# The attention slot of a transformer kernel: masks from the fifth score round on, ScalarE's copies ahead of the output, the input transposed behind the output projection

## The reference, cut to what matters

```
x = x + 0.5 * L0_ffn(layernorm(x))
x = x + L0_attn(layernorm(x))
x = x + 0.5 * L0_ffn(layernorm(x))
x = x + 0.5 * L1_ffn(layernorm(x))
x = x + L1_attn(layernorm(x))
x = x + 0.5 * L1_ffn(layernorm(x))
```

```
h = shift_token(x)                       # half of the channels come from the row before
q, k, v = split(h @ wqkv)                # 8 heads of 64
q = l2norm(q) * qs; k = l2norm(k) * ksc
q, k = rotary_xpos(q, k)
# windows of 128 rows; a row sees its own window and the one before, at most 128 rows back
sim  = (8 q) @ k^T                       # 128 queries x 192 keys for half a window
attn = softmax(where(mask, -max, sim))
x = x + (attn @ v) @ wo
h = layernorm(shift_token(x)) @ w1 + b1
x = x + (a * gelu(g)) @ w2 + b2
```

## Time and profile before

| | us |
|---|---|
| median of 3 runs (lowest, highest) | 3214.93 (3213.61, 3220.47) |
| the profiled execution: its own time | 3218.03 |
| the profiled execution: its span | 3216.0 |
| TensorE busy | 3018.5 (94% of the span) |
| VectorE busy | 2361.8 (73%) |
| ScalarE busy | 1721.1 (54%) |
| GpSimd busy | 1671.5 (52%) |

### The profile page before, as it was taken

The page is one execution under the profiler, slowest core; times in us unless marked ns, Lnnn a source line. Parts: engine busy times, 40 slices in busy tenths (PEclk is TensorE's granted clock), DMA queues, the critical chain, the costliest instruction groups (busy, mean ns, idle before and its releaser), DMA issues.

```text
span 3216.0 us, 98899 instructions
## 1 busy us (share of the span) xinstructions
PE 3018.5 (94%) x35586; PEld 2604.5 (81%) x35586; DVE 2361.8 (73%) x6543; ACT 1721.1 (54%) x4532; POOL 1671.5 (52%) x1839
## 2 busy tenths in 40 slices
PE   6999989989999999999899999999999899999889
PEld 4777878878887888998688878877888788898778
DVE  6777777677777786777677777767777688777766
ACT  4666652266667324665676763237666622454445
POOL 7777740077777224323777771037777444317610
PEclk9999999999999999999999999999999999999999
DMA  4211121021111101000211112102111200100001
GB/s 146 58 42 39 38 81 36 23 62 39 37 38 37 45 20 42 10 11 21 57 39 37 38 37 78 29 25 66 37 38 35 66 26 13 27 1 1 1 14 39
DMA packets 178773, 122.82 MB, mean 38 GB/s; under 512 B 27532, under 2 KB 175336, under 8 KB 178024
## 3 DMA queue, kind: packets, MB, share of 16 engines
q1 hardware_dynamic: 177432, 117.77, 13.6%
q10 hardware_dynamic: 1104, 1.90, 0.2%
HBM read 48.29 MB, written 20.98 MB: 22 GB/s over the span
## 4 chain that ended last, share of the span: by engine, by line
PE 62%; ACT 18%; issue 8%; DVE 8%; DMA 1%; POOL 1%; DVEq 1%; SPq 0%; ACTq 0%; POOLq 0%
ACT prob L1247 14%; PE bank L363 7%; PE bank L365 5%; PE scores L508 5%; PE bank L364 5%; PE scores L363 4%; PE scores L364 4%; PE scores L365 4%; PE bank L478 2%; PE pair_bank L770 2%; PE pair_bank L769 2%; PE pair_bank L768 2%; ACT V L1231 2%; PE scores L714 2%; PE scores L713 2%
## 5 line engine op out<-in xcount | busy, mean ns | idle before, releaser
L2699 POOL TENSOR_TENSOR prob<-prob,rsum 128x384 f32<-128x384 f32 x512 | 467.5, 933 | 282.6 <-DVE rsum L1900 267.2
L1247 ACT ACTIVATE prob<-prob,nmax 128x192 f32<-128x192 f32 x1024 | 452.0, 443 | 290.5 <-DVE nmax L1893 290.4
L1440 ACT ACTIVATE gate<-scores,bias 128x512 f32<-128x512 f32 x192 | 132.2, 689 | 511.4 <-PE scores L365 511.4
L2686 POOL TENSOR_TENSOR rn<-ss,mhalf 128x16 f32<-128x16 f32 x128 | 375.2, 2931 | 10.7
L363 PE MATMUL bank<-wqkv_hi,hT_hi 128*128 128x512 f32 x768 | 338.9, 441 | 8.7 <-DVE hT_lo L1833 3.7
L2693 POOL TENSOR_TENSOR qk<-rot_t 128x512 f32<-128x512 f32 x256 | 322.6, 1278 | 36.1 <-DVE ss L1867 29.7
L2667 POOL TENSOR_TENSOR rstd<-meanvar,eps 128x4 f32<-128x4 f32 x48 | 11.1, 231 | 627.2 <-DVE meanvar L1825 627.2
L1893 DVE CUSTOM_DVE_ANT_0 prob<-scores,masks,rn 128x192 f32<-128x192 f32 x768 | 267.7, 412 | 84.4 <-PE scores L508 83.9
L365 PE MATMUL bank<-wqkv_hi,hT_lo 128*128 128x512 f32 x768 | 305.7, 398 | 0.0
L364 PE MATMUL bank<-wqkv_lo,hT_hi 128*128 128x512 f32 x768 | 302.5, 394 | 0.0
L1853 DVE TENSOR_TENSOR rot_t<-bank,rot 128x512 f32<-128x512 f32 x256 | 176.1, 688 | 163.8 <-ACT qk L1224 156.2
(11 more groups left out here) (338 smaller groups left out, 9662.6 us busy)
## 6 DMA issues: line engine op xcount, KB each, us to landing
Vlo<-V SPq DMA_DIRECT2D x256, 64.0 KB, 2.0
Vhi<-V SPq DMA_DIRECT2D x256, 64.0 KB, 2.0
H<-Y SPq DMA_DIRECT2D x128, 64.0 KB, 1.8
H<-ya SPq DMA_DIRECT2D x128, 64.0 KB, 1.9
yb<-Y SPq DMA_DIRECT2D x128, 64.0 KB, 1.6
HB<-Y SPq DMA_DIRECT2D x32, 256.0 KB, 2.8
HB<-yb SPq DMA_DIRECT2D x32, 256.0 KB, 3.0
raw<-in_L_ffn_wqkv SPq DMA_DIRECT2D x4, 1536.0 KB, 6.9
```

The costliest lines, as they stand in the source:

```text
L1247: ins = e.activation(pb, pb, ACT.Exp, bias=nm[r][:, x:x + 1], scale=-1.0, accum_out=sums[r][:, x:x + 1])
L2686: e.tensor_tensor(rn[u][:, :], ss[:, :], mhalf[:, :], ALU.pow).then_inc(s_plRN, 1)
L2699: e.tensor_tensor(pair, pair, rs[:, 2 * gi:2 * gi + 2].unsqueeze(2).to_broadcast([P, 2, KW]), ALU.mult).then_inc(s_plPN[gi], 1)
```

## The change: what it does

1. **Masks earlier, and one semaphore for all of them.** TensorE counts up a new semaphore `s_peSA` with the last matmul of the fifth of the eight score rounds. By then everything that is written to bank 2 is there (heads 4, 6 and half of head 0). VectorE's `sc_` now waits for `s_peSA` before the first mask and for `s_peS` (all rounds) before the third. The waits for the four transposes of the slot before (`s_pePT`), which stood one before each block, all stand ahead of the first mask now. Each mask counts up `s_dvMX` by itself, and each exponential waits for its own mask and counts up `s_acEX` by itself.
2. **Another order of heads.** Blocks 1 and 2 change places in `PAIRS`; the order of masks and exponentials is that of `EXP_ORDER`. `TURN_BANK` and the order of the transposes, products and copies of the blocks follow.
3. **ScalarE copies qT, V and the input ahead of the output.** `ot_` moves from behind the exponentials to behind the kT copy, and waits also for `hT_lo` of tile T+3.
4. **The input is transposed behind the output projection**, ahead of the q transposes, and into the upper half of bank 6 in place of bank 1. `pv_` waits also for the `hT_lo` that last read that bank.
5. The k projection waits for bank 1 itself, since the input's transposes no longer do it.

```diff
-PAIRS = [(0, 4), (1, 5), (2, 6), (3, 7)]
+PAIRS = [(0, 4), (2, 6), (1, 5), (3, 7)]
+EXP_ORDER = (((0, 1), (1, 1), (0, 0), (1, 0)), ((2, 0), (3, 0), (2, 1), (3, 1)))
-TURN_BANK = (3, 2, 2, 4)
+TURN_BANK = (2, 3, 4, 2)
@@ input_bank @@
-            return bank[2 + T] if spare(run, T) else bank[1]
+            if spare(run, T):
+                return bank[2 + T]
+            return bank[1] if isinstance(T, int) and T < 3 else bank[6][:, 2 * P:4 * P]
@@ TensorE @@
+                                if half_ == 1 and h == 0 and piece == 0:
+                                    ins.then_inc(s_peSA, 1)
...
-                    if gi == 1:
-                        e.wait_ge(s_dvMX[2], G + 1 + OFF)
-                    if gi == 2:
-                        e.wait_ge(s_acPT[1], G + 1 + OFF)
+                    if gi == 0:
+                        e.wait_ge(s_dvMX[2], 2 * G + 2 + OFF)
+                        e.wait_ge(s_dvMX[3], 2 * G + 2 + OFF)
+                    if gi == 3:
+                        e.wait_ge(s_acPT[0], G + 1 + OFF)
@@ TensorE pv_ @@
+                    if inside(T + 3):
+                        e.wait_ge(s_dvHT, G + 4 + OFF)
@@ TensorE slot @@
                         wo_(T - 2, (u - 2) % U)
+                    if inside(T + 3):
+                        ht(T + 3, (u + 3) % U)
                     if inside(T + 1):
                         tr_(T + 1, (u + 1) % U, 0)
                     if inside(T + 2):
                         v_(T + 2, (u + 2) % U)
-                    if inside(T + 3):
-                        ht(T + 3, (u + 3) % U)
@@ ScalarE sc_ @@
-                    e.wait_ge(s_dvMX[gi], G + 1 + OFF)
-                    for i in range(2):
+                    for n, (gi, i) in enumerate(EXP_ORDER[hf]):
...
+                        e.wait_ge(s_dvMX[gi], 2 * G + 1 + n // 2 + OFF)
@@ ScalarE ot_, now behind tr_(T + 1, ..., 1) @@
+                    if inside(T + 4):
+                        e.wait_ge(s_dvHT, G + 5 + OFF)
@@ VectorE sc_ @@
-                    e.wait_ge(s_peS, G + 1 + OFF)
+                    e.wait_ge(s_peSA, G + 1 + OFF)
...
-                    e.wait_ge(s_pePT[gi], G + OFF)
-                    e.sem_inc(s_passed, 1)
+                    for g in range(NG):
+                        e.wait_ge(s_pePT[g], G + OFF)
+                        e.sem_inc(s_passed, 1)
...
+                        if n == 2:
+                            e.wait_ge(s_peS, G + 1 + OFF)
+                            e.sem_inc(s_passed, 1)
```

More of the change, by code:

```diff
@@ L416, in ht @@
                     into = input_bank(run, T)
-                    if not spare(run, T) and not (isinstance(T, int) and T == 0):
+                    if run == DEPTH and isinstance(T, int) and 1 <= T < 3:
                         k_read(T - 1)
@@ L441, in qk_ @@
                         q_read(T - 1)
-                    elif j == 1 and spare(run, T):
+                    elif j == 1 and (not early or spare(run, T)):
                         k_read(T - 1)
@@ L544, in product @@
                         return e.matmul(bank[6 + i][cols, o0:o0 + DH], keys[x][rows, h * DH:(h + 1) * DH], PTs[gi][rows, p0:p0 + DH], start=start, stop=x < 2, skip_group_check=True)
-                    for hf in range(2):
+                    for n in range(2):
                         for x in (2, 3):
-                            for g in range(2):
+                            for gi in (n, n + 2):
                                 for i in range(2):
-                                    product(2 * hf + g, i, x, slice(DH * i, DH * i + DH), hf == 0 and x == 2)
-                    for hf in range(2):
+                                    product(gi, i, x, slice(DH * i, DH * i + DH), n == 0 and x == 2)
+                    for n in range(2):
                         for i in range(2):
                             for x in (0, 1):
-                                for g in range(2):
-                                    ins = product(2 * hf + g, i, x, slice(0, P), False)
-                        ins.then_inc(s_pePV[hf], 1)
+                                for gi in (n, n + 2):
+                                    ins = product(gi, i, x, slice(0, P), False)
+                        ins.then_inc(s_pePV[n], 1)
                 def wo_(T, u):
@@ L1267, in slot @@
                     if inside(T):
+                        sc_(T, u, 0)
                         sc_(T, u, 1)
-                        sc_(T, u, 0)
-                        sc_(T, u, 3)
-                        sc_(T, u, 2)
-                    if inside(T - 1):
-                        ot_(T - 1, (u - 1) % U)
                     if inside(T + 1):
@@ L1280, in slot @@
                     if inside(T):
+                        pt_(T, u, 0)
                         pt_(T, u, 1)
-                        pt_(T, u, 0)
                     if inside(T + 1):
                         tr_(T + 1, (u + 1) % U, 1)
+                    if inside(T - 1):
+                        ot_(T - 1, (u - 1) % U)
                     if inside(T + 3):
@@ L1287, in slot @@
                     if inside(T):
+                        pt_(T, u, 2)
                         pt_(T, u, 3)
-                        pt_(T, u, 2)
                 def iteration(it):
@@ L1887, in sc_ @@
                         e.sem_inc(s_passed, 1)
-                    for i in range(2):
+                    for n, (gi, i) in enumerate(EXP_ORDER[0] + EXP_ORDER[1]):
+                        if n == 2:
+                            e.wait_ge(s_peS, G + 1 + OFF)
+                            e.sem_inc(s_passed, 1)
                         x = 2 * gi + i
@@ L2701, in mask_of @@
                 def mask_of(it):
-                    e.wait_ge(s_dvMX[2], NT * run + U * it - U + 1 + OFF)
-                    e.wait_ge(s_dvMX[3], NT * run + U * it - U + 1 + OFF)
+                    e.wait_ge(s_dvMX[2], 2 * (NT * run + U * it - U + 1) + OFF)
+                    e.wait_ge(s_dvMX[3], 2 * (NT * run + U * it - U + 1) + OFF)
                     odd = it - 2 * (it // 2)
@@ L2723, in slot @@
                     if inside(T):
+                        pn_(T, u, 0)
                         pn_(T, u, 1)
-                        pn_(T, u, 0)
+                        pn_(T, u, 2)
                         pn_(T, u, 3)
-                        pn_(T, u, 2)
                     if inside(T + 2):
```

33 lines of the change are left out of this document (14 added, 19 removed).

## The result

The changed kernel takes 3184.16 us (median of 4 runs, 3179.62 to 3187.18); the kernel before took 3217.7 beside it (3213.61 to 3222.32, 4 runs). The ratio is 0.9894, 95% interval 0.9874 to 0.9914: faster, as forecast, but by 34 us and not by 99. The time lies outside the range of 3102 to 3158. The profiled execution took 3187.18 (span 3185.4), 30.8 less than that of before; clock 0.990 against 0.993.

A forecast was written before the change was run, and what follows sets the result against it. TensorE was taken as leading, losing 0.91 per slot to waits for the V copy and `hT_lo`. 112 full slots x 0.83 (93 us) plus 5 or 6 from edge slots, together 98.5, gave 3116 us, range 3102 to 3158.

The forecast's parts named there:

- the chain: Within a slot, scores, masks, exponentials, output, qT, V, input, `hT_lo` follow one another; shortening it by 0.90 removes both TensorE waits.
- 0.48 + 0.34 + 0.08 = 0.90: Per-slot gain at the V copy: output moved 0.48, exponentials waiting for their own mask 0.34, earlier masks 0.08.
- Two transposes move, none is added: On TensorE, moving the input's transposes was taken as free; only the further wait at `pv_` was charged, 0.05.
- The output costs nothing behind kT: On ScalarE, the 0.48 output fits the 0.97 gap ahead of the square of q; at most 0.48 if not.
- rival A: VectorE's waits ahead of the masks cost 0.23 each, so masks start 0.25 later than before: 3149 us, 12%.
- rival C: VectorE's masks slow down reading PSUM while scores are written; at a pitch of 0.68, 3338 us, 4%.
- The new semaphore: Signalled to VectorE after the fifth score round, some 0.45 to 0.5 earlier; net mask gain 0.08 after more waits.
- Rival B: GpSimd's third product goes ahead of VectorE's scaling of k, delaying the q projection: 3187 us, 6%.
- the collision: VectorE's scaling of k starts in the tail of GpSimd's second product in every slot, losing 0.18 at most.
- the 0.3 to spare: VectorE's scaling of k was to end at +7.05, in time for the k transposes by 0.3.
- rival D: No change: something outside the rows read holds TensorE as long as the V copy did; about 3215 us, 3%.
- The ceiling: TensorE's two waits, for the V copy and `hT_lo`, lose 0.91 per slot, the most a regular slot could gain.

The follow-up runs named there:

- The third and fourth experiments: Changed kernel with the input's transposes behind the V projection again: 3163.12 us; changed kernel without the `hT_lo` wait ahead of the products with V: 3171.97 us.
- the fifth: Changed kernel with the input's transposes behind the V projection again and without the `hT_lo` wait ahead of the products with V: 3155.31 us.
- the last experiment: Changed kernel without `pv_`'s `hT_lo` wait, V projection ahead of output projection, V copied first, and without VectorE's four `s_pePT` waits ahead of the masks: 3116.6 us.
- the kernel with V ahead: Changed kernel without the `hT_lo` wait at the products with V, and with V projected and copied ahead of q's transposes and copy: 3124.1 us.
- The three fastest kernels: Changed kernel without `pv_`'s `hT_lo` wait, V projection ahead of q transposes (3124.1 us), ahead of output projection (3118.82), or that without four mask waits (3116.6).

## Why the prediction was wrong

*The step that failed* is the sentence that closes the chain: "0.48 + 0.34 + 0.08 = 0.90. V is out, and the k transposes allowed, at +8.04 - 0.90 = +7.14". It followed the V copy back along ScalarE only. The copy has a second input, TensorE's V projection, and its end wasn't in the sum. The trace of before has it, in the slot of the earlier trace rows:

```profile
877.09 0.40 PE L365 MATMUL bank<-wqkv_hi,hT_lo 128*128 128x512 f32 x1
```

It ends at 877.49, 0.60 before V is copied (878.09). So even with TensorE's order untouched V could not gain 0.90. The list of waits of before hid this, since ScalarE came later than TensorE in all but 9 slots.

*The second failed step* is "Two transposes move, none is added", with 0.05 for the wait. Both edits lie ahead of the V projection: the transposes push its end back by 0.22, the wait by 0.13. By the medians of the table V was forecast at 7.31 - 0.90 = 6.41 and came at 7.00. Of these 0.59, the old end of the projection accounts for 6.64 + 0.03 - 6.41 = 0.26, the transposes and the wait for 0.33 together (6.64 to 6.97). The third and fourth experiments took those two back one by one (0.22 and 0.13), the fifth both, with V at +6.65, the place that the old projection end allows.

*What held.* The output costs nothing behind kT: moved alone, it gave 0.47 of its 0.48. First masks were forecast at +1.95 and the first exponential at +2.41; they came at +1.92 and +2.38. Each exponential waits for its own mask, and the waits ahead of the masks cost 0.115 each, as the last experiment shows, so rival A is out. The masks keep their pitch of 0.34 (884.01, 884.36), so rival C didn't come. It wasn't put to a real test, though: the scores' 64 matmuls, which take 1.57 from the slot's start, are over ahead of the first mask at +1.92; only in the last kernel (+1.46) does a mask begin beside them, for 0.11, and the pitch there is 0.35. The new semaphore itself came as forecast: in the changed kernel's trace VectorE passes the wait for it at +1.19, where it passed the one for all scores at +1.64 before. Rival B is out: the scaling starts inside the second product, and the third doesn't go first. The scaling takes 0.76 in the median, not 0.69. The view of one line over the whole span (ns min, median, max), beside the earlier trace rows, and GpSimd's timeline in slot 882.10, beside the earlier trace rows:

```profile
L1880 DVE TENSOR_TENSOR qk<-qk,rn x128: 679/760/1582, 32.5 to 2500.8; 128x512 f32<-128x512 f32 x128
```

```profile
886.98 3.63 POOL L2706 TENSOR_TENSOR prob<-prob,rsum 128x384 f32<-128x384 f32 x4 [1.86 <-DVE rsum L1910]
```

So the collision costs 0.07; the 0.3 to spare covered it. The Trainium skill (SBUF — State Buffer, Who interferes with whom) has the rule of an exclusive lock, under which the product that came first would hold the scaling until its own end. That product starts at +5.66, takes 0.83 and ends at +6.49, and the scaling starts at +6.28, so an estimate by that rule is 0.21 + 0.69 = 0.90 for the scaling. The trace agrees in direction and shows a third of that delay.

*The rivals.* By its number rival B (3187) is 3 us from the measured time, but that is chance: its mechanism didn't come. By its mechanism rival D, "something outside these rows", was the nearest: it got 3%, and had no row named.

*The size of it.* The 112 full slots took 1401.8 in sum before and 1364.6 after: 37.2 less where 93 were forecast. The rest of the program took 6.4 more, in place of 5.5 less: edge slots 2.3 less, the three stretches between the passes 5.2 more (954.6 to 959.8), start and last part 3.6 more. Those stretches are 3 to 9 longer in each of the ten other profiles. The granted clock goes with part of it: the start took 39.3 at a clock of 1.00 before and 41.1 at 0.96 after, the first stretch between passes 228.4 at 1.00 and 232.0 at 0.99. Why the clock was lower there, and the rest of the difference, stays open.

*The ceiling was right, and a little low.* With V and `hT_lo` out of the way a slot takes 11.31 to 11.32, where 11.46 was forecast and 11.39 the best case. From the q projection to the next slot's scores it is 11.31 - 7.70 = 3.61 there, 3.63 in the earlier trace rows. The full slots of the kernel with V ahead sum to 1303.1, 98.7 less than before, where 93 was forecast. The three fastest kernels take 94 to 100 us less in time than the kernel before, where the prediction had 99. So the forecast gain was there to be had; the change as made stopped 60 to 68 us short of these.

Some slots in the faster kernels are long for another reason. In the changed kernel one of them shows at TensorE's products with V:

```profile
2183.23 0.34 PE L552 MATMUL pair_bank<-probT,Vlo 64*64 64x64 f32 x8 [1.92 <-DMA Vhi<-V]
```

That is in the slot at 2179.74, which took 14.12. In the kernel with V ahead, four full slots take 13.2 to 15.9. TensorE stands idle in each of them ahead of or within the products with V: 1.62 and 2.77 for that DMA in two, 1.87 and 2.36 with no releaser named in the other two. In the three longest, the mean granted clock of the slot is 0.89 where other slots have 1.00. The longest of them, with its idle time, its window, and two us behind the idle time (length; busy us of PE, PEld, DVE, ACT, POOL; clock):

```profile
2133.36 0.34 PE L550 MATMUL pair_bank<-probT,Vlo 64*64 64x64 f32 x8 [2.77 <-DMA Vhi<-V]
```

```profile
2129.02:2144.87 15.85, 13.08 (x181) 11.53 (x180) 9.02 (x31) 8.80 (x27) 10.94 (x10) 0.89 0.22 50
2135.00:2137.00 2.00, 2.00 (x19) 1.88 (x16) 1.82 (x5) 0.80 (x4) 2.00 (x3) 0.50 0.14 34
```

So behind the idle time TensorE ran, in those two us, at the lower of its two clock levels, 1.2 GHz in place of 2.4. No run takes the idle times away, so what they cost in all stays open.

## What to carry to other kernels

A wait names only the last of the inputs. Before counting a gain on a chain, look up when each other input of the same instruction comes ready, at its place in the new order, and cap the gain there: here one more row of the timeline, 0.60 ahead of the copy, would have cut the sum from 0.90 to about 0.6. A wait that has left the list isn't gone either: look whether the gap in the timeline has gone with it. Then treat each instruction moved ahead of such an input as a cost of its full pitch (0.11 for a transpose, 0.12 for a wait that is already met), even where "none is added". And what an edit is worth depends on the limit of the day: the early masks were worth nothing in the changed kernel and 23 us once V was ahead.

## What was not expected of the hardware

- A semaphore wait that is already met isn't free on TensorE: one cost 0.12 per slot here, some 12 us of 3184; on VectorE four of them cost 0.46. In the traces such waits stand 0.11 to 0.12 apart on both engines.
- The busy time of TensorE in a slot isn't a floor. The changed kernel shows 11.87 busy in 12.00 and looks full; the same matmuls run in 11.31 with V ahead. The ends of matmuls are modelled, and small gaps between them are counted in. The gaps in the timeline (0.40 to the k transposes where 0.11 is the pitch) told what the share of busy time didn't.
- A scaling on VectorE and a product on GpSimd that meet stretch one another, but the price hardly depends on where they meet: the third product takes 1.29 in the kernel before and 1.27 in the changed one (medians of the 112 full slots; alone 0.83), and the scaling 0.69 and 0.76.
